# A last batch without a next one: expert weights split beside the output projection, whole scatters, and products that change nothing ahead of the experts

## What is computed

```python
h = tokens(x)                                       # (4, 749, 192)
h = h + attention(layernorm(h))                     # ends with z @ W_O + b_O
xt = layernorm(h).reshape(-1, 192)
expert_idx = argmax(softmax(xt @ gate_w + gate_b))  # one of 8 experts for each token
for e in range(8):
    y = gelu(xt @ w1[e] + b1[e]) @ w2[e] + b2[e]    # w1: 192 x 768, w2: 768 x 192
    out = where(expert_idx == e, y, out)
h = h + out
```

## Time and profile before

| | |
|---|---|
| median of three runs | 1709.54 us (1706.84 to 1710.92) |
| the profiled execution | 1712.28 us, of which 1710.5 us are its span |
| busy: PE, DVE, ACT, POOL | 1467.2, 1097.5, 774.2, 421.1 us |
| granted TensorE clock, mean over the span | 0.919 of 2.4 GHz |
| fourth batch: last transposes of the last pair of heads end | 1477.0 us |
| first transposes of the expert stage | 1550.62 us |
| load of a tile from the slots (line 695), issue to landing | 1.9 us |
| ACT's copy of the second token transposes (line 1074) | 0.79 us |
| sample preparation on DVE (lines 1342 to 1345) in the fourth batch, start to end | 1477.94 to 1487.82 us |
| the same in the first batch | 372.37 to 374.64 us |

### The profile page before, as it was taken

The page is one execution under the profiler, slowest core; times in us unless marked ns, Lnnn a source line. Parts: engine busy times, 40 slices in busy tenths (PEclk is TensorE's granted clock), DMA queues, the critical chain, the costliest instruction groups (busy, mean ns, idle before and its releaser), DMA issues.

```text
span 1710.5 us, 31540 instructions
## 1 busy us (share of the span) xinstructions
PE 1467.2 (86%) x10354; PEld 989.7 (58%) x10355; DVE 1097.5 (64%) x2502; ACT 774.2 (45%) x1491; POOL 421.1 (25%) x433
## 2 busy tenths in 40 slices
PE   5987699998987899999977999999877999927997
PEld 4433477785343577784433777764335777824665
DVE  5988545458987455559885555569875555735554
ACT  2654455534563555525643455426544555223332
POOL 3000233313000233303001333220002565721222
PEclk6998899998988899998998999979988999957999
DMA  4996122210000222201000221100002433211221
GB/s 115 342 354 203 36 47 56 53 27 28 12 0 1 56 50 60 50 4 39 1 0 9 64 64 45 37 25 16 1 1 75 109 96 95 67 34 31 63 66 32
DMA packets 115156, 105.39 MB, mean 62 GB/s; under 512 B 57401, under 2 KB 105594, under 8 KB 115073
## 3 DMA queue, kind: packets, MB, share of 16 engines
q1 hardware_dynamic: 83570, 55.32, 13.5%
q10 hardware_dynamic: 25744, 39.62, 7.1%
q0 software_dynamic: 5760, 9.36, 1.7%
HBM read 30.05 MB, written 47.28 MB: 45 GB/s over the span
## 4 chain that ended last, share of the span: by engine, by line
PE 48%; DVE 30%; issue 12%; ACT 5%; POOL 3%; DMA 2%; POOLq 0%; DVEq 0%; SPq 0%; ACTq 0%
PE ps L1864 13%; DVE arena L1298 9%; PE ps L1915 8%; DVE arena L1296 5%; PE ps L1838 5%; PE ps L1850 5%; PE ps L1806 5%; DVE bn L1431 4%; PE ps L1961 2%; DVE arena L1325 2%; PE ps L1813 2%; ACT arena L1017 1%; POOL out L908 1%; DVE nmax L1317 1%; PE ps L1872 1%
## 5 line engine op out<-in xcount | busy, mean ns | idle before, releaser
L1915 PE MATMUL ps<-arena,cwt 128*128 128x504 f16 (+2 forms) x1776 | 392.4, 382 | 38.5 <-DVE arena L1296 36.3
L1915 PEld LDWEIGHTS ps<-arena,cwt 128*128 128x128 f16 x1776 | 176.1, 102 | 255.2 <-DVE arena L1296 39.9
L1317 DVE TENSOR_REDUCE nmax<-ps 128x1 f32<-128x128 f32 (+5 forms) x288 | 176.9, 614 | 177.3 <-PE ps L1841 177.3
L1864 PE MATMUL ps<-arena 128*128 128x64 f32 (+2 forms) x2016 | 259.6, 269 | 8.2 <-DVE arena L1325 4.8
L1864 PEld LDWEIGHTS ps<-arena 128*128 128x128 f32 (+2 forms) x2016 | 241.3, 188 | 25.0 <-issue 13.9
L1298 DVE TENSOR_TENSOR arena<-arena 128x1008 f16<-128x1008 f32 (+4 forms) x200 | 227.0, 1135 | 6.9
L1325 DVE COPY arena<-ps 128x512 f32<-128x512 f32 (+4 forms) x288 | 155.8, 541 | 84.2 <-PE ps L1850 79.8
L976 ACT ACTIVATE arena<-ps,nmax 128x128 f32<-128x128 f32 (+5 forms) x288 | 180.3, 626 | 39.6 <-DVE nmax L1317 38.8
L1838 PE MATMUL ps<-arena 128*128 128x512 f16 (+6 forms) x780 | 164.1, 314 | 29.5 <-ACT arena L1017 16.4
L1033 ACT ACTIVATE arena<-ps 128x1008 f32<-128x1008 f32 (+1 forms) x112 | 96.1, 866 | 180.3 <-PE ps L1915 180.3
L1850 PE MATMUL ps<-ident,arena 128*128 128x128 f32 (+2 forms) x1008 | 165.2, 281 | 11.0 <-ACT arena L1017 6.0
(11 more groups left out here) (287 smaller groups left out, 2351.3 us busy)
## 6 DMA issues: line engine op xcount, KB each, us to landing
slot_scratch<-empty_slot ACTq DMA_DIRECT2D x1, 38692.5 KB, 120.8
arena<-arena SPq DMA_DIRECT2D x96, 187.5 KB, 2.9
arena<-arena SPq DMA_DIRECT2D x96, 93.8 KB, 2.3
arena<-in_L_ffn_w SPq DMA_DIRECT2D x16, 288.0 KB, 4.6
arena<-in_L_ffn_w SPq DMA_DIRECT2D x8, 576.0 KB, 6.1
arena<-slot_scratch SPq DMA_DIRECT2D x31, 96.5 KB, 1.9
arena<-slot_scratch SPq DMA_DIRECT2D x31, 96.0 KB, 1.9
xa<-in_x POOLq DMA_DIRECT2D x5, 468.8 KB, 4.3
```

The costliest lines, as they stand in the source:

```text
L1317: v.reduce_max(nmax[0:m, k_:k_ + 1], slot(g)[0:m, 0:128 * i + m], AX.X, negate=True).then_inc(S["smax_done"], 1)
L1864: last = t.matmul(slot(g)[0:m, Z_AT:Z_AT + DH], probt[k % 2][0:kk, c, 0:m], vt[0:kk, c, DH * hh:DH * hh + DH], start=c == 0, stop=c == i)
L1915: last = t.matmul(bank(g, k)[:, 0:c * PITCH].rearrange("p (r c) -> p r c", c=PITCH), cwt[layer][:, w, tap, :], parts[x][:, f:f + 2 * c - 1 ...
```

## The change

- A phase LAST_POST is added for the last batch: the jobs wo, wo, tr, tr, gate, gate, rank alone. POOL loads no samples in the fourth batch's tower, and DVE does no `split_samples` there.
- DVE and ACT split w1b, w1a and b2 within LAST_POST: on DVE, after the six additions of b_O and ahead of the take of the projection, come eight `w1b_low`, `b2_both` and `w1a_low(0)`, `w1a_low(1)`; `w1a_low(2)` comes after the variance, and `w1a_low(3)` to `(7)` after the take of the first transposes. On ACT, eight `w1b_high` and six `w1a_high` stand ahead of its copy of the second transposes, and two behind it. w1a gets one region with five places ahead in place of two regions, and one semaphore for each expert's load.
- All scatters have 128 rows. The 19 rows past the tokens of the sixth go to 128 new rows past the end of the slots (TRASH_ROW), by numbers written once at the start; DVE writes the slot numbers in two instructions in place of one.
- POOL makes the expert stage's three constants after the gate, ahead of the scatters. ACT ends with an activation of the GELU that the experts use.
- PE issues 16 such products ahead of its wait for the last batch's layer norm and 30 ahead of the first tile of the experts.

```diff
+def last_post_jobs():
+    return [job for job in post_jobs() if job[0] in ("wo", "tr", "gate", "rank")]
...
-                load_samples((b + 1) & (BATCH - 1))
+                if b < BATCH - 1:
+                    load_samples(b + 1)
...
+            const(g.iota(slots[:, :], pattern=[[0, TT]], base=TRASH_ROW, channel_multiplier=1))
...
                 for t in range(TT):
-                    rows = SEQ - 128 * (TT - 1) if t == TT - 1 else 128
                     pool.indirect_dma_start(out=slot_dram,
-                                            out_offset=bass.IndirectOffsetOnAxis(ap=slots[0:rows, t:t + 1], axis=0),
-                                            in_=token_rows[0:rows, t, :], in_offset=None
+                                            out_offset=bass.IndirectOffsetOnAxis(ap=slots[:, t:t + 1], axis=0),
+                                            in_=token_rows[:, t, :], in_offset=None
                                             ).then_inc(S["scattered"], 16)
...
+            def w1a_high(e):
+                act.wait_ge(w1a_loaded[e], 16)
+                if e >= W1A_AHEAD:
+                    act.wait_ge(w1a_split, e + 1 - W1A_AHEAD)
+                a.activation(w1a_parts[0:HALF + 1, e, 0:FF], w1a_raw[0:HALF + 1, e + W1A_AHEAD, :], ACT.Copy,
+                             scale=WSCALE).then_inc(w1a_made, 1)
...
+                if b == BATCH - 1:
+                    for e in range(EXPERTS):
+                        w1b_high(e)
+                    act.wait_ge(biases_loaded, 32)
+                    for e in range(6):
+                        w1a_high(e)
...
+                if b < BATCH - 1:
+                    split_samples(POST, b)
                 for i in range(TT):
                     m = tile_rows(i)
                     last = v.tensor_tensor(h[0:m, i, :], h[0:m, i, :], bo_b[0:m, :], ALU.add)
                 step(last)
+                if b == BATCH - 1:
+                    for e in range(EXPERTS):
+                        w1b_low(e)
+                    b2_both()
+                    for e in range(2):
+                        w1a_low(e)
...
                     elif kind == "tr":
                         v.tensor_copy(xnt0[:, 0:TOK], slot(g)[:, 0:TOK]).then_inc(S["dve_freed"], 1)
+                        if b == BATCH - 1:
+                            for e in range(3, EXPERTS):
+                                w1a_low(e)
...
-                        v.tensor_copy(slots[:, :], slots_f[:, :]).then_inc(S["slots_ready"], 1)
+                        v.tensor_copy(slots[:, 0:TT - 1], slots_f[:, 0:TT - 1])
+                        v.tensor_copy(slots[0:LASTM - 1, TT - 1:TT], slots_f[0:LASTM - 1, TT - 1:TT]
+                                      ).then_inc(S["slots_ready"], 1)
...
                         if args[0] == 0:
+                            if b == BATCH - 1:
+                                keep_busy(g, 16)
                             wait(pe, "xn_ready", post, 1, b)
...
             pe.wait_ge(b2_split, 2)
+            keep_busy(0, 30)
             make_xt(0, 0)
```

More of the change, by code:

```diff
@@ new lines @@
+    "affine_ready": (1, CONV_LAYERS - 1, 0, 0, 1, 0),
+    "norm_done": (0, sum(len(c) for c in NORM_CHUNKS.values()) + 1, 0, 0, 0, 0),
+    "hi_done": (0, len(SPLITS), 0, 0, 0, 0),
+    "lo_done": (0, len(SPLITS), 0, 0, 0, 0),
+    "halo_done": (0, 4, 0, 0, 0, 0),
+    "xn_ready": (0, 1, 0, 0, 1, 1),
+    "w_loaded": (288, 144, 144, 0, 0, 0),
+    "w_split": (1, 1, 1, 0, 0, 0),
+    "w_step": (1, 1, 1, 0, 0, 0),
+    "ln_scaled": (0, LN_PARTS, 0, 0, 0, 0),
+    "xn_high": (0, LN_PARTS, 0, 0, 0, 0),
@@ L247, in at @@
     setup, *each = COUNTS[sem]
-    tower, pair, last_pair, post = each
+    tower, pair, last_pair, post, last_post = each
     before_last = tower + (PAIRS - 1) * pair
@@ L253, in at @@
     if phase == MOE:
-        return setup + BATCH * period + k
+        return setup + BATCH * period - post + last_post + k
     base = b * period + setup
@@ L540, in audio_tower @@
         expert_loaded = [sem(f"expert_loaded_{e}") for e in range(EXPERTS)]
-        w1a_loaded, b2_loaded = sem("w1a_loaded"), sem("b2_loaded")
+        w1a_loaded = [sem(f"w1a_loaded_{e}") for e in range(EXPERTS)]
+        biases_loaded = sem("biases_loaded")
         w2_step, w2_split, b2_split = sem("w2_step"), sem("w2_split"), sem("b2_split")
@@ L830, in tower_and_first_weights, with moe_const, moe_consts_made, end_of_batch @@
                 split_weights(TOWER, b)
-            def end_of_batch(b):
-                wait(pool, "var_ready", POST, 1, b)
+            def moe_const(ins_):
+                steps[0] += 1
+                ins_.then_inc(moe_consts, 1)
+                pool.wait_ge(moe_consts, steps[0])
+            def moe_consts_made():
+                wait(pool, "ps_full", LAST_POST, job_index(LAST_POST, "gate", (1,)) + 1, BATCH - 1)
+                steps[0] = 0
+                for par in range(2):
+                    moe_const(g.memset(x_parts[par][HALF:HALF + 1, 0, 0, :], 1.0))
+                moe_const(g.iota(part_no, pattern=[[0, 1]], base=0, channel_multiplier=1,
+                                 allow_small_or_imprecise_dtypes=True))
+                assert steps[0] == N_MOE_CONSTS
+            def end_of_batch(b, phase=POST):
+                wait(pool, "var_ready", phase, 1, b)
                 g.tensor_tensor(lnr[:, :], lnv[:, :], neg_half[:, 0:TT], ALU.pow).then_inc(S["rstd_ready"], 1)
-                group_rstd(POST, 2, b)
+                if phase == POST:
+                    group_rstd(POST, 2, b)
+                else:
+                    moe_consts_made()
                 pool.wait_ge(slots_cleared, 16)
-                wait(pool, "slots_ready", POST, 1, b)
+                wait(pool, "slots_ready", phase, 1, b)
                 g.tensor_tensor(carry[:, 0:1], ones_col[:, :], ones_col[:, :], ALU.mult
@@ L881, in _ @@
                 w2_low(e)
-            end_of_batch(BATCH - 1)
-            wait(pool, "ps_full", MOE, 0)
+            end_of_batch(BATCH - 1, LAST_POST)
             wait(pool, "rows_free", MOE, 0)
[L886 to L891, removed]
-            for par in range(2):
-                moe_const(g.memset(x_parts[par][HALF:HALF + 1, 0, 0, :], 1.0))
-            moe_const(g.iota(part_no, pattern=[[0, 1]], base=0, channel_multiplier=1,
-                             allow_small_or_imprecise_dtypes=True))
-            assert steps[0] == N_MOE_CONSTS
             def scatter_out(i, par, first=False):
@@ L1247, in final_layernorm @@
                 meanwhile()
-                wait(dve, "rstd_ready", POST, 1, state["b"])
+                wait(dve, "rstd_ready", state["phase"], 1, state["b"])
                 token_norms(range(TT)).then_inc(S["xn_ready"], 1)
@@ L1495, in _ @@
                         else:
-                            final_layernorm(lambda: samples_job(POST, job_index(POST, "xt", (0,)), b))
-                            wait(dve, "xn_ready", POST, 1, b)
+                            final_layernorm((lambda: w1a_low(2)) if b == BATCH - 1 else
+                                            lambda: samples_job(POST, job_index(POST, "xt", (0,)), b))
+                            wait(dve, "xn_ready", post, 1, b)
                             step(v.tensor_copy(token_rows[:, :, 2 * D:ROW].bitcast(i32), token_no[:, :].unsqueeze(2)))
@@ L2004, in make_hidden @@
                     pe.wait_ge(gelu_done, j - 1)
-                high_low = [[parts[0:rows, bass.ds(e, 1), :].rearrange("p a f -> p (a f)") for parts in pair]
-                            for rows, pair in ((HALF + 1, (w1a_high, w1a_low)), (HALF, (w1b_parts,)))]
-                a_high, a_low = high_low[0]
-                b_both = high_low[1][0]
+                a_both, b_both = (parts[0:rows, bass.ds(e, 1), :].rearrange("p a f -> p (a f)")
+                                  for rows, parts in ((HALF + 1, w1a_parts), (HALF, w1b_parts)))
                 for k in range(2):
```

189 lines of the change are left out of this document (91 added, 98 removed).

## The result

The changed kernel took 1687.05 us as the median of 4 runs (1685.65 to 1688.70), the kernel before 1708.88 beside it: a ratio of 0.9874, 95% interval 0.9855 to 0.9893. The profiled execution took 1688.44 us with a span of 1686.7. Its mean granted clock is 0.931, before 0.919.

The account below looks back on a forecast made before the run. The expert stage is bound by PE, its cost set by when it starts and how warm. Starting 16.9 us earlier, plus 3.1 for the clock, minus 0.3 in earlier batches, gives 19.7: median 1689.8 us, own range 1685 to 1694, whole 1680 to 1698.

Parts of the forecast that it names:

- the start of the stage: Expert stage in the last batch: starts at 1533.7 in place of 1550.6, 16.9 us earlier.
- wait of POOL's power beside a split: Before the last layer norm: w1a_low(2) gets the shared ports just ahead of POOL's power, which waits some 0.75 us.
- The splits beside the projection: Last batch's output projection: DVE takes turns with POOL's w2 splits, reaching the projection's result 8.1 us late, at 1497.9.
- Rival A: Output projection: ports don't hold DVE back, additions and splits done at 1489.6, gain 28.9, 1681 us; chance 0.12.
- The gate: Last batch's gate on PE: twelve products take 5.0 us, between 3.9 with the clock rising at once and 6.2.
- The bound of 6.2: Gate's twelve products, 24 records, all at half clock, worked from 13 records in 3.1 us.
- The whole scatter in the last batch: Sixth scatter with 128 rows: landed at slots + 10.1 in place of + 20.6, gain 10.5 us.
- The thirty products: Ahead of the experts: 9.3 us (bounds 6.6 and 12.9), about what the tile load needs, and they raise PE's clock.
- rival C: Ahead of the experts: the thirty products don't raise the clock, gain 13.3 - 0.3, 1696.5 us; chance 0.08.
- At full clock: ... = 6.4. Gain 3.1: Expert stage's start: first transposes to the hidden's first transposes takes 6.4 us in place of 9.5.
- D's mechanism: Expert stage: the clock falls again within it, up to 4.67 us more a tile, 1713 with five; chance 0.02.
- The earlier batches hide both the scatters and the gain; the one more copy costs them 3 x 0.1: Three earlier batches: whole scatters bring nothing there, and the second slot copy costs 0.3 us in all.

Follow-up runs that it names:

- w2_early: Changed kernel with all of POOL's w2 splits placed within the last batch's head pairs, so POOL is idle when DVE adds b_O: 1679.73 us, 0.9806.
- kb62: Changed kernel with 62 products in place of 16 ahead of PE's wait for the last layer norm: 1686.60 us, 0.9838.
- all_fills: w2_early plus gap_fill's products, six products ahead of the gate, and 34 in place of 16 ahead of the token transposes: 1676.43 us, 0.9799.
- scatter109: Changed kernel with the sixth scatter of every batch back at 109 rows: 1699.78 us, 0.9923 to the kernel before.
- whole_last: Kernel before with whole_alone's edits, but the sixth scatter has 128 rows in the last batch only, 109 in earlier ones: 1698.63 us, 0.9935.
- gap_fill: Changed kernel with four more products behind the experts' first tile's transposes and three behind the second's: 1686.26 us, 0.9862.
- whole_alone: Kernel before with only the 128-row scatters, their spare rows, one more iota and the slot copy in two pieces: 1693.78 us, 0.9899.
- two_adds: Changed kernel with the six additions of b_O done in two instructions: 1687.95 us, 0.9881.

## Why the prediction was right, step by step

In the last batch the mechanism forecast is the one the trace shows; 1687.05 stands against 1689.8. That the number came so near is in part luck, since terms missed in opposite directions: the start of the stage gave 16.4 for 16.9, its clock 1.2 for 3.1, and what lies ahead of the last batch gave 6.1 where it was to cost 0.3.

| step, from the last bias | forecast | measured |
|---|---|---|
| additions of b_O end | +11.0 | +10.3 |
| take of the projection | +20.9 | +20.1 |
| wait of POOL's power beside a split | 0.75 us | 0.58 |
| gate's products | 5.0 us | 6.2 |
| slot numbers | +43.2 | +43.5 |
| POOL free, behind the slot numbers | 10.1 us | 10.15 |
| thirty products | 9.3 us | 9.10 |
| experts' first transposes | +56.7 | +57.2 |
| from there to the hidden's | 6.4 us | 8.3 |
| all that lies before the last bias | 0.3 later | 6.1 earlier |

- The splits beside the projection: right, and w2_early shows the cause by taking it away. Rival A falls: with POOL idle DVE comes to the projection at +12.5, as that rival had it for POOL busy.
- The gate: I took a clock that rises in its midst. It lay at the bound of all at half. The 11.6 us that PE idles ahead of the transposes are not the only reason: kb62 takes them away and the gate still takes 6.2 us; with products in the gap behind the transposes as well, all_fills takes 3.7. The bound of 6.2 was right but misread: 13 records in 3.1 us would make 5.7 for 24, and one of the 13 is the end of another product. The slot numbers came out right because the take was 0.8 us early and the gate 1.2 late.
- The whole scatter in the last batch: right in size (10.6 us of POOL's time) and cause (scatter109, whole_last).
- The thirty products: they took what was forecast and raised the clock, so rival C falls as it was put. The term that failed is "At full clock: ... = 6.4. Gain 3.1". It gained 1.2, because the clock fell again, behind transposes and hand-overs that leave PE busy for 0.63 of 2.3 us. Such a stretch doesn't always bring the fall, as w2_early and kb62 show. gap_fill, where the clock stayed up, measures the term at 6.8. D's mechanism, a fall within the stage, is therefore real, from 1531 to 1534 and not for five tiles: from 1545 on the trace has full clock, as the earlier trace rows.
- "The earlier batches hide both the scatters and the gain; the one more copy costs them 3 x 0.1": failed. What lies ahead of the last bias gave 6.1 us in the profiled pair, and some 6 by the medians of whole_alone and, with 109 rows, of scatter109. 0.7 of it is traced to the scatter; the rest goes with a clock level whose cause stays open, and so does the part of the whole scatters in it.

In sum: 16.4 us from the earlier start, 1.2 from the clock, 0.1 behind it and 6.1 ahead of it are the 23.8 us between the two profiled executions. The medians are 21.8 apart. No run leaves out the splits or the constants alone, so their shares of the 16.4 are not measured one by one.

## What to carry to other kernels

Before work is put beside a free engine, look at what its neighbour on the shared ports does in those microseconds: here moving POOL's work away made the tail another 8.9 us shorter. A transfer's partition count can cost more than its bytes: 19 useless rows made the tail 11 us shorter. Useless products can lose what they bought when sparse work follows before the dense work: here thirty of them gave 0.2 us in all. So look at the clock's windows behind them as well as under them, and in more than one execution.

## What was not expected of the hardware

- A DVE cast with one input took 1.39 us in place of 0.67 beside an indirect scatter's issue on POOL (2.89 us for 109 rows beside a busy DVE; 1.53 for 128).
- The waits go both ways: in two_adds a w2 instruction of POOL took 2.90 us in place of 2.11 beside the longer additions, and another 2.97 in place of 2.37 beside the splits of w1b.
- The same sparse stretch, PE busy for 0.63 of 2.3 us, was followed by a fall of the clock to half in the changed kernel and by none in w2_early.
- 62 products, over 13.5 us, did not carry the clock over the 4.3 us behind them, of which PE was busy for 1.61.
- Each of the three batches takes one of two times, some 2.9 us apart, and the same kernel shows both.
